# Dummy matmuls in the idle stretches of TensorE, and another order of the sampling work, in a fused block of deformable convolution, attention and experts

## The reference, cut to what matters

```
xg = group_norm(x)                                  # statistics of each image and channel
x_proj = xg @ w_in + b_in
x1 = gelu(layer_norm(depthwise_conv3x3(xg) + dw_b) * ln_g + ln_b)
offset = x1 @ w_off + b_off                         # 8 groups x 9 points x 2
mask   = softmax((x1 @ w_msk + b_msk) over the 9 points of a group)
sampled = sum over points of mask * bilinear(x_proj, pixel + point + offset)
x = x + sampled @ w_out + b_out
t = tokens(x);  t = t + attention(layer_norm(t));  t = t + top2_of_8_experts(layer_norm(t))
```

## Time and profile before

| | |
|---|---|
| median of 3 runs | 107.4 us (107.09 to 108.33) |
| profiled execution, its own time | 108.61 us |
| its span in the trace | 106.9 us |
| busy share: TensorE, VectorE, GpSimd, ScalarE | 73, 63, 41, 29% |
| mean granted clock of TensorE in the trace's clock row | 0.837 |

### The profile page before, as it was taken

One profiled execution on the slowest core, in us unless ns is written; L12 is line 12 of the kernel. 1 busy time (PEld: TensorE's weight loads), 2 busy tenths in 40 slices (PEclk: granted clock), 3 DMA queues, 4 the chain that ended last, 5 costly groups with the idle time before them and its releaser, 6 DMA issues.

```text
span 106.9 us, 1448 instructions
## 1 busy us (share of the span) xinstructions
PE 78.2 (73%) x533; PEld 65.0 (61%) x533; DVE 67.1 (63%) x127; ACT 30.8 (29%) x66; POOL 44.1 (41%) x73
## 2 busy tenths in 40 slices
PE   3797999489801995599399965979448899957820
PEld 3696499389602994599399954956124588933400
DVE  2046200427968999907828934882997268989990
ACT  0441000696991410100740002154934130101100
POOL 6019999700526999999300000000003300494440
PEclk9999999999985599859999999999975555695555
DMA  0214300028400000000000000000000000000022
GB/s 26 83 32 92 62 8 0 6 65 257 123 0 3 0 0 0 0 0 6 3 0 0 0 0 3 6 0 0 0 0 0 0 6 0 0 0 0 3 46 53
DMA packets 5115, 2.36 MB, mean 22 GB/s; under 512 B 4290, under 2 KB 4643, under 8 KB 5107
## 3 DMA queue, kind: packets, MB, share of 16 engines
q1 hardware_dynamic: 4675, 2.06, 8.1%
q10 hardware_dynamic: 432, 0.20, 0.7%
HBM read 0.81 MB, written 0.26 MB: 10 GB/s over the span
## 4 chain that ended last, share of the span: by engine, by line
PE 40%; DVE 35%; ACT 11%; issue 6%; DMA 3%; DVEq 1%; POOL 1%; POOLq 0%
DVE image_all L936 8%; PE ps L580 7%; PE ps L492 7%; PE ps L532 5%; DVE prod L288 4%; DVE att_d L1084 4%; DMA x_rows<-in_x 3%; ACT absoff L777 2%; DVE image_all L1132 2%; PE ps L592 2%; ACT hat L781 2%; PE ps L692 2%; PE ps L522 2%; PE ps L654 2%; DVE prod L1167 2%
## 5 line engine op out<-in xcount | busy, mean ns | idle before, releaser
L580 PE MATMUL ps<-wide_ident,prod 128*128 128x128 f32 x81 | 13.0, 334 | 9.5 <-DVE prod L288 9.5
L580 PEld LDWEIGHTS ps<-wide_ident,prod 128*128 128x128 f32 x81 | 12.2, 178 | 10.3 <-DVE prod L288 5.6
L936 DVE TENSOR_TENSOR image_all<-ps,images 128x1024 f32<-128x1024 f32 (+3 forms) x8 | 14.2, 1818 | 6.4 <-PE ps L580 6.4
L492 PE MATMUL ps<-wide_ident 128*128 128x128 f32 x70 | 14.4, 367 | 1.8 <-POOL wide_ident L367 1.8
L492 PEld LDWEIGHTS ps<-wide_ident 128*128 128x128 f32 x70 | 12.8, 270 | 4.0 <-issue 2.2
L476 POOL TENSOR_TENSOR prod<-prod,tok 128x256 f32<-128x256 f32 x2 | 1.9, 964 | 30.3 <-DVE prod L1091 30.3
L592 PE MATMUL ps<-wide_ident,image_all 128*128 128x128 f32 x100 | 12.0, 274 | 0.0
L592 PEld LDWEIGHTS ps<-wide_ident,image_all 128*128 128x128 f32 x100 | 11.0, 141 | 0.2 <-DVE image_all L936 0.2
L483 POOL TENSOR_TENSOR image_all<-image_all 128x512 f32<-128x512 f32 (+1 forms) x6 | 6.0, 1008 | 11.1 <-DVE image_all L1132 10.9
L284 POOL TENSOR_TENSOR my<-prob,hat 128x384 f32<-128x384 f32 x8 | 7.8, 1000 | 2.3 <-DVE ps L284 2.3
L288 DVE TENSOR_TENSOR prod<-ps,hat 128x1152 f32<-128x1152 f32 x6 | 7.9, 1351 | 0.4 <-ACT ps L797 0.3
(11 more groups left out here) (171 smaller groups left out, 131.4 us busy)
## 6 DMA issues: line engine op xcount, KB each, us to landing
images<-images SPq DMA_DIRECT2D x2, 300.0 KB, 4.1
images<-images SPq DMA_DIRECT2D x2, 280.0 KB, 3.5
x_tok<-in_x SPq DMA_DIRECT2D x4, 64.0 KB, 2.3
out_dram<-prod SPq DMA_DIRECT2D x3, 64.0 KB, 2.2
x_rows<-in_x SPq DMA_DIRECT2D x1, 128.0 KB, 2.7
x_rows<-in_x ACTq DMA_DIRECT2D x1, 128.0 KB, 3.1
expert<-in_expert_w SPq DMA_DIRECT2D x4, 32.0 KB
out_dram<-prod ACTq DMA_DIRECT2D x1, 64.0 KB, 2.5
```

Source lines behind the costliest of these rows:

```text
L492: pe.matmul(pbank(bank, P), ident, ident, start=True, stop=True)
L580: ins = pe.matmul(coef_rows(ty, tx, tx + 1), prod[:, ky, dy, kx * D + dx, :], ident, start=first[tx // 4], stop=((ky, dy) == PAIRS_OF_ROW[ ...
L936: v.tensor_tensor(taps[:, ty % SLOTS, t0:t1, :, :], bcast(coef_rows(ty, t0, t1).rearrange("p (t j) -> p t j", j=P), 2, GC), images[:, t0:t ...
```

## The change

The numbers of dummy matmuls in the prologue go from 3, 3, 2, 1 to 5, 5, 4, 1, and those after the transposes of x move behind `vec_T`. A new run of 26 stands between the projections and the first sum of the sampling. `ln_T` moves from before the convolution to behind it, and the copy that reads it on ScalarE likewise. In the sampling, both the order of weights and products on VectorE and the order of pairs, sums and taps on TensorE are written anew; the flag's matmul, the flag and the reciprocal `rden` move forward, the transposes of the image for `x_proj` and its copy backward.

```diff
--- before.py
+++ after.py
@@ -45,7 +45,7 @@
 HP = H + 2 * PADY
 VECTOR_PAIRS = ((0, 0), (0, 1), (1, 0), (0, 2), (1, 1), (1, 2))
 POOL_PAIRS = ((2, 0), (2, 1), (2, 2))
-PAIRS_OF_ROW = tuple(tuple((ky, ty - ky) for ky in range(K) if 0 <= ty - ky < D) for ty in range(TW))
+PAIRS_OF_ROW = (((0, 0),), ((0, 1), (1, 0)), ((0, 2), (2, 0), (1, 1)), ((2, 1), (1, 2)), ((2, 2),))
 PIECES = (((0, 2), (2, 5)), ((0, 5),), ((0, 5),), ((0, 5),), ((0, 2), (2, 4), (4, 5)))
 HALVES = 2
 GA = 2
@@ -58,7 +58,7 @@
 LOG_EXP = "natural_log_exp_and_others"
 OUT_OF_RACE = -1e30
 
-WARM = {"start": 3, "group sums": 3, "squares": 2, "normalised": 1, "layer norm": 0,
+WARM = {"start": 5, "group sums": 5, "squares": 4, "normalised": 1, "hats": 26, "layer norm": 0,
         "projection weights": 1, "token norm": 12, "lnT": 2, "second norm": 3,
         "second norm, last group": 6, "ln2T": 2}
 
@@ -340,6 +340,7 @@
             sp.wait_ge(flag_ready, 1)
             far = sp.value_load(flag[0:1, 0:1], min_val=0, max_val=1)
             with sp.If(far > 0):
+                sp.wait_ge(x_proj_ready, 1)
                 sp.dma_start(image_dram, x_proj[:, :]).then_inc(img_stored, 16)
                 sp.wait_ge(img_stored, 16)
                 sp.wait_ge(taps_used, TW)
@@ -498,10 +499,10 @@
             for b in range(4):
                 ins = pe.transpose(pbank(4, P, b * P), x_rows[:, b * P:(b + 1) * P], ident)
             ins.then_inc(xT_done, 1)
-            keep_warm(7, WARM["group sums"])
             pe.wait_ge(vec_in, 2 * 16)
             pe.transpose(pbank(1, NP + 1), vec_rows[:, :, :].rearrange("r q c -> r (q c)"),
                          ident[0:NP + 1, 0:NP + 1]).then_inc(vec_T, 1)
+            keep_warm(7, WARM["group sums"])
 
             def over_segments(at, even, odd):
 
@@ -515,8 +516,6 @@
             keep_warm(7, WARM["squares"])
             pe.wait_ge(x_segments, 1)
             over_segments(64, x_segvar[:, :, 0], x_segvar[:, :, 1]).then_inc(x_var, 1)
-            pe.wait_ge(ln_in, 2 * 16)
-            pe.transpose(pbank(5, 2), ln_rows[:, :, :].rearrange("r q c -> r (q c)"), ident[0:2, 0:2]).then_inc(ln_T, 1)
             pe.wait_ge(vec_cols_ready, 2)
             pe.wait_ge(centring_ready, 1)
             pe.matmul(pbank(2), conv_bias[:, :], bcast(centring[0:C, :], 1, W), start=True, stop=False,
@@ -533,6 +532,8 @@
                                     xnT[:, b, dy:dy + H, :], conv_w[:, dy, lo:hi, :],
                                     start=False, stop=(b == 3 and dy == K - 1), skip_group_check=True)
             ins.then_inc(conv_done, 1)
+            pe.wait_ge(ln_in, 2 * 16)
+            pe.transpose(pbank(5, 2), ln_rows[:, :, :].rearrange("r q c -> r (q c)"), ident[0:2, 0:2]).then_inc(ln_T, 1)
 
             pe.wait_ge(ones_ready, 1)
             pe.wait_ge(w_in_ready, 1)
@@ -595,23 +596,26 @@
                                             skip_group_check=True)
                 ins.then_inc(taps_used, 1)
 
+            pe.wait_ge(upper_ready, 1)
+            pe.wait_ge(lower_ready, 1)
+            keep_warm(SPARE, WARM["hats"])
             add_weights(0)
             add_weights(1)
             add_taps(0)
             add_weights(2)
+            pe.wait_ge(over_ready, 1)
+            pe.matmul(ps[0:1, SPARE, 0:1], over_all[:, :], ones[:, 0:1], start=True, stop=True).then_inc(flag_sum, 1)
             add_taps(1)
+            add_weights(3)
+            add_weights(4)
+            add_taps(2)
+            pe.wait_ge(flag_ready, 1)
             for c in range(GC):
                 ins = pe.transpose(pbank(SPARE, P, c * P), image[:, c, :], ident)
             ins.then_inc(image_T, 1)
-            add_weights(3)
-            add_taps(2)
-            add_weights(4)
             add_taps(3)
-            pe.wait_ge(over_ready, 1)
+            add_taps(4)
             pe.wait_ge(x_proj_ready, 1)
-            pe.matmul(ps[0:1, SPARE, 0:1], over_all[:, :], ones[:, 0:1], start=True, stop=True).then_inc(flag_sum, 1)
-            add_taps(4)
-            pe.wait_ge(flag_ready, 1)
             for half, bank in enumerate((SPARE, 0)):
                 pe.wait_ge(samp_ready, half + 1)
                 for b in range(2):
@@ -751,10 +755,10 @@
             act.activation(conv_bias[:, :], ones[0:C, :], ACT.Copy, scale=vec_cols[0:C, 0:1]).then_inc(vec_cols_ready, 1)
             act.wait_ge(x_var, 1)
             inv_sqrt(gn_rstd[:, :], gn_ln[:, :], pbank(0, NI, 64), eps[:, 0:1], 1.0).then_inc(gn_rstd_ready, 1)
+            act.wait_ge(conv_done, 1)
+            act.activation(c_sq[:, :], pbank(2), ACT.Square).then_inc(conv_squared, 1)
             act.wait_ge(ln_T, 1)
             act.activation(ln_cols[:, :], pbank(5, 2), ACT.Copy).then_inc(ln_cols_ready, 1)
-            act.wait_ge(conv_done, 1)
-            act.activation(c_sq[:, :], pbank(2), ACT.Square).then_inc(conv_squared, 1)
             act.wait_ge(conv_summed, 1)
             inv_sqrt(c_rstd[:, :], c_ln[:, :], c_sum[:, :], eps[:, 1:2], 1.0 / C).then_inc(conv_rstd_ready, 1)
             act.preload_act_table(ACT.Gelu)
@@ -789,20 +793,24 @@
                     exponentials(ch + 1)
                     act.wait_ge(upper_ready, ch + 2)
 
-            for i in range(1, len(VECTOR_PAIRS)):
+            def keep_rows(i):
+
                 ky, dy = VECTOR_PAIRS[i]
                 act.wait_ge(my_made, i)
                 if i >= 2:
                     act.wait_ge(vector_weighted, i - 1)
                 act.activation(my_bank(i), my[:, ky, dy], ACT.Copy).then_inc(my_ready, 1)
 
-            act.wait_ge(image_T, 1)
-            act.activation(x_proj[:, :].rearrange("p (j c) -> p c j", c=GC), pbank(SPARE).rearrange("p (c j) -> p c j", c=GC),
-                           ACT.Copy).then_inc(x_proj_ready, 1)
+            for i in range(1, 5):
+                keep_rows(i)
             act.wait_ge(middle_ready, NCH - 1)
             act.wait_ge(last_hats, 1)
             act.activation(absoff[:, :, :], absoff[:, :, :], ACT.Relu,
                            bias=minus_one[:, :], accum_out=over_all[:, :]).then_inc(over_ready, 1)
+            keep_rows(5)
+            act.wait_ge(image_T, 1)
+            act.activation(x_proj[:, :].rearrange("p (j c) -> p c j", c=GC), pbank(SPARE).rearrange("p (c j) -> p c j", c=GC),
+                           ACT.Copy).then_inc(x_proj_ready, 1)
 
             act.wait_ge(samp_T, 1)
             act.activation(sampT[:, :, :, 0:2].rearrange("p n y b -> p b y n"),
@@ -962,17 +970,17 @@
             weights(2)
             v.wait_ge(img_in, 4 * 16)
             products(0)
-            products(1)
             weights(3)
             weights(4)
+            products(1)
+            weights(5)
             products(2)
-            weights(5)
+            v.wait_ge(flag_sum, 1)
+            v.tensor_scalar(flag[:, :], ps[0:1, SPARE, 0:1], 0.0, None, ALU.is_gt).then_inc(flag_ready, 1)
             products(3)
-            products(4)
             v.wait_ge(den_ready, 1)
             v.reciprocal(rden[:, :], den[:, :]).then_inc(rden_ready, 1)
-            v.wait_ge(flag_sum, 1)
-            v.tensor_scalar(flag[:, :], ps[0:1, SPARE, 0:1], 0.0, None, ALU.is_gt).then_inc(flag_ready, 1)
+            products(4)
             v.wait_ge(flag_ready, 1)
             far = v.value_load(flag[0:1, 0:1], min_val=0, max_val=1)
             with v.If(far > 0):
```

## The result

The changed kernel takes 96.85 us in the median of 4 runs (96.10 to 97.79), beside 107.87 us (4 runs, 107.09 to 110.94) for the kernel before: a ratio of 0.898, 95% interval 0.886 to 0.910. Some executions of either kernel are over 1.5% slower than its fastest, and every ratio here leaves them out: one of each kernel in this pair (97.79 and 110.94 us). The forecast was 99.6 us with a range down to 97.5, so the kernel is faster than the range allowed. Its profiled execution is the fastest of the four, 96.10 us with a span of 94.4.

What follows compares the result with a forecast made beforehand. No engine is full, so order and waiting were taken to set the time. From 108.6 us, 5.8 (sampling) and 2.6 (prologue) off gave 100.2, less 0.6 for the median's lead: 99.6 us, range 97.5 to 103.2.

Steps and rivals of the forecast that it cites:

- Prologue: Start to the convolution's end: more dummies bring the full clock earlier, ending it at 15.95 instead of 18.86; 2.6 us taken.
- From the means' sums to the variance's: Stretch of the prologue before the convolution: 2.6 us instead of 2.8, by faster weight loads.
- From the variance's sums to the end of `xnT`: Last prologue stretch before the convolution: 2.36 us as before, ending at 12.3.
- Convolution at the full clock: Convolution in the prologue: all at the full clock, 3.6 us, from 12.35 to 15.95.
- Bias and dummy: TensorE work just before the convolution: at the full clock it ends at 12.0, hidden, where it took 2.6 us.
- Hats: Between projections and sums: 26 dummies take 6.4 us and make the first sum 1.1 late, which nobody feels.
- Sampling: First weights to `samp`: the new order removes VectorE's waits and moves `rden` off the end; `samp` at 58.25, 5.8 us gained.
- Token stage: After the sampling: nothing changes but the clock's chance, allowed 1.2 us either way.
- the median's lead: Median lies 1.2 us below the profiled execution of the kernel before; half, 0.6 us, carried over to the forecast.
- (a): Prologue: full clock does not hold and dummies only delay, 0.5 us lost instead of 2.6 gained; 102.7 us, chance 0.28.
- (b): Sampling: one arrival given slack comes late and half the gain stays away; 102.5 us, chance 0.08.
- (c): Sampling: a run of transposes does not hold the full clock, so slower than before; 111.6 us, chance 0.04.

Runs made afterwards that it cites:

- e4: Kernel before with one edit, the transposes of the taps ahead of the three prologue dummies: ratio 0.996 to the kernel before.
- e9_changed: The changed kernel again with no edit, on another chip: median 97.56 us, ratio 0.899 to the kernel before.
- e10: Changed kernel with 5 + 5 dummies in the attention and the image transposes and their copy ahead of the sums: median 94.52 us, ratio 0.868.
- e3: Kernel before with only the 26 dummies in the hats added: ratio 1.001 to the kernel before.
- e5: Changed kernel without the 26 dummies in the hats: ratio 0.892 to the kernel before.
- e8: Changed kernel with 5 + 5 dummies in the attention and 6 ahead of the transposes of `c_norm`: median 94.98 us, ratio 0.874.

## Why the prediction was wrong, by its own steps

**Prologue, 2.6 us forecast, 4.2 measured (means of nine executions with the new prologue and three with the old; 5.0 between the first two profiles): the term that was mis-sized most.** Its steps added up to 2.9, of which 2.6 were taken, and the largest error that every execution shows is in one of them. From the means' sums to the variance's 2.6 us were set down, and 1.57 measured, 1.34 to 1.63 in the nine. The forecast took 0.2 off the old 2.8 for faster weight loads. But that 2.8 held 0.9 us in which VectorE was held up beside GpSimd's products (0.87 and 0.38 us where e4 has 0.17 and 0.17), and moving `vec_T` removed 0.76 of that in the first profile. I had costed the move at nothing, on TensorE alone; that it pulls `conv_w` away from the square was in rows that I had not read side by side. The first sums themselves took 0.59 us where 1.03 had stood, 0.4 less where 0.2 had been taken off; the dummies around them took 0.26 and 0.25 us each, where the first five of the kernel took 0.50.

The other steps, in the first profile: the means' sums should have begun at 7.35 and began at 6.33. The transposes took 0.7 us and not 1.1, and the five dummies 1.31 and not 1.75: at 0.26 us each, they were fast from the first. That is the part that is luck: in e9_changed the dummies took 1.85 us and the sums began at 7.04, in e10 at 7.57. From the variance's sums to the end of `xnT` 2.36 were set down and 1.95 measured (9.85 - 7.90), of which 0.4 are the sums: 0.61 us where 1.01 had stood. Together 12.35 became 9.99, or 10.47 in e9 and 11.09 in e10. The convolution took 3.83, not 3.6, in all nine.

**Convolution at the full clock**: right: 8 records in 1.00 us (11.0 to 12.0), where the first 8 of before took 2.00. Bias and dummy took 1.05 and 0.42 us; they were forecast as hidden and end 0.13 us after `xnT`, so they are on the chain for that much. `ln_T` behind the convolution: right, it costs nothing (its copy ends at 14.51, VectorE's sum at 15.17).

**Hats, 0 us**: right. The 26 dummies took 5.97 us (6.4 forecast), and products(0) starts 4.84 us after the first row weights, as before (37.03 - 32.19). e3 and e5 show that they could be left out.

**Sampling, 5.8 forecast, 6.49 measured**: the mechanism was right but for its last step: VectorE's wait of 0.41 us for the sums of ty = 3 (0.3 forecast), 111 transposes in 12.35 us (12.4). The 0.65 us come in four parts, counted from the first row weights. 0.25: the forecast let the flag's register read begin after products(4) and had `samp` wait for it; `samp` waits for TensorE, as e10 shows by taking four transposes away. 0.18: 0.2 was set down for handing over, and 0.02 measured (54.16 to 54.18). 0.17: taps(1) began that much earlier than forecast. 0.05: the transposes. That the read is partly covered is shown by e10; under what it lies is not.

**Token stage, 0 with 1.2 either way**: too narrow for one execution, where it is 0 or 2.5 us; prologue and sampling (4.2 and 6.5) make 10.7 of the 11.0 us between the medians, so little is left for it there. The 0.6 us of the median's lead is within that same chance.

The sum mended: 99.6 - 1.6 (the prologue, 4.2 in place of 2.6) - 0.65 = 97.35, against medians of 96.85 and 97.56. Neither term alone takes the sum out of the range, and both together only just (97.5); the other 0.5 us is within the 1.7 us by which single executions lie apart.

**Rivals.** (a), the clock falls back in the prologue: in none of the nine profiled executions with the new prologue; the convolution took 3.83 us in each. (b), half of the sampling's gain: no. (c), transposes lose the clock: no; it stayed at 1.00 through all 111 of them, which took 12.35 us.

## What to carry to other kernels

An instruction that is moved also moves its consumers on other engines: list what runs beside them before and after, since here a product of GpSimd held up a VectorE square that has no semaphore to do with it (0.87 us before, 0.17 in e4). Where one engine waits for sums whose inputs come in a fixed order, write down both queues with their durations and issue inputs in the order in which the sums are closed; here that took 6.5 us out of one stretch. Dummy matmuls paid here only where a chain of waits ran over TensorE while it was slow (convolution records at 0.25 us each, the token stage at a granted clock of 0.50): in front of the convolution (3.6 us, together with the moves of `vec_T` and `ln_T`) and in the token stage (2.6 us), not in the hats (nothing).

## What was not expected of the hardware

In the kernel before, the clock row reads 1.00 from the start although 8 records of the convolution took 2.00 us there and 1.00 later: its first entries can't be taken for a measurement. The same program has its clock at 0.50 from 18.4 to 21.7 us in one execution and from 68.2 to 78.0 in another, so two profiles differ by 2.5 us in one stage (23.82 and 26.28). The same prologue ends up to 1.1 us apart (13.81 to 14.95), by when its matmuls become fast: the five dummies behind `vec_T` took 1.31 us in the one (e8) and 2.38 in the other (e10). A stage has to be compared over several executions. And VectorE's 0.17 us square took 0.22, 0.28, 0.45 or 0.87 us, depending on when a product of GpSimd beside it ended.
